# A state-space scan whose inputs come from TensorE, whose weighing by C is GpSimd's, and whose C is spread by DMA

## The reference, cut to what matters

```
Bx = xc @ B_w.T ; Cx = xc @ C_w.T            # 64 states each, per position
dt = softplus(xc @ dt_w.T + dt_b) + 0.0001
h  = exp(dt_t * A) * h + (dt_t * x_t) * Bx_t   # per position t, for all (d, n)
y  = einsum('bdn,bn->bd', h, Cx_t) + D_param * x_t
y  = y * silu(z)
```

## Time and profile before

| | us |
|---|---|
| median of 3 runs | 8258.76 (8253.63 to 8259.18) |
| the profiled execution | 8256.86 |
| its span | 8255.1 |
| TensorE busy in the span | 6220.3 (75%) |
| VectorE busy | 6656.1 (81%) |
| ScalarE busy | 3462.9 (42%) |
| GpSimd busy | 3679.6 (45%) |

### The profile page before, as it was taken

The page is one execution under the profiler, slowest core; times in us unless marked ns, Lnnn a source line. Parts: engine busy times, 40 slices in busy tenths (PEclk is TensorE's granted clock), DMA queues, the critical chain, the costliest instruction groups (busy, mean ns, idle before and its releaser), DMA issues. The chain is left out here.

```text
span 8255.1 us, 122802 instructions
## 1 busy us (share of the span) xinstructions
PE 6220.3 (75%) x40740; PEld 4162.2 (50%) x40740; DVE 6656.1 (81%) x11381; ACT 3462.9 (42%) x6666; POOL 3679.6 (45%) x1911
## 2 busy tenths in 40 slices
PE   5455555799966677777777777777778879999999
PEld 3355554577755422222222222222245558888888
DVE  6799998555557899999999999999955557676766
ACT  3333332333323566666666666666534421111121
POOL 0000000111100599999999999999822212222222
PEclk8777777899988899999999999999989989999999
DMA  2211111111022100000000000000011110000000
GB/s 64 73 43 43 43 43 52 43 37 37 28 79 108 66 15 15 15 15 15 15 15 15 15 15 15 15 15 15 12 57 46 40 63 8 7 8 8 7 8 6
DMA packets 335678, 254.48 MB, mean 31 GB/s; under 512 B 161763, under 2 KB 307046, under 8 KB 334854
## 3 DMA queue, kind: packets, MB, share of 16 engines
q1 hardware_dynamic: 332774, 248.29, 9.7%
q10 hardware_dynamic: 2464, 0.26, 0.0%
HBM read 140.46 MB, written 108.00 MB: 30 GB/s over the span
## 5 line engine op out<-in xcount | busy, mean ns | idle before, releaser
L1817 POOL TENSOR_TENSOR ss_inp<-ss_dx,ss_b_all 128x1024 f32<-128x1024 f32 x1024 | 2388.8, 2356 | 230.8 <-ACT ss_b_all L1791 229.0
L1835 DVE TENSOR_TENSOR_SCAN ss_h<-banks,ss_inp 128x1024 f32<-128x1024 f32 x1024 | 2313.1, 2278 | 59.7 <-ACT banks L1783 59.7
L1755 PE MATMUL banks<-ss_ch,ident 128*128 128x512 f32 x4096 | 1959.6, 601 | 64.9 <-DVE ss_xc L1851 64.9
L1733 PE MATMUL banks<-ss_bc,ss_pick 96*128 96x512 bf16 x2048 | 747.2, 386 | 787.9 <-DVE ss_ch L1844 750.4
L1783 ACT ACTIVATE banks<-ss_dt,ss_neg_a 128x510 f32<-128x510 f32 x2048 | 1334.7, 688 | 2.7 <-DVE ss_h L1835 2.7
L1791 ACT COPY ss_b_all<-banks 128x512 f32<-128x512 f32 x1024 | 599.3, 585 | 1236.5 <-PE banks L1733 1232.8
L1755 PEld LDWEIGHTS banks<-ss_ch,ident 128*128 128x128 f32 x4096 | 788.7, 193 | 635.1 <-issue 577.6
L1733 PEld LDWEIGHTS banks<-ss_bc,ss_pick 96*128 (+1 forms) x2048 | 200.0, 98 | 1662.7 <-issue 1484.7
L1844 DVE TENSOR_TENSOR ss_ch<-ss_h,banks 128x1024 f32<-128x1024 f32 x768 | 918.0, 1195 | 0.0
L605 PE MATMUL banks<-ms_rprod,ident 128*128 128x128 f32 x2048 | 467.0, 401 | 507.6 <-DVE ms_rprod L691 507.6
L2156 POOL TENSOR_TENSOR pk_blockhot<-pk_onehot,pk_parts 128x2048 bf16<-128x2048 bf16 x96 | 345.4, 3626 | 1101.0 <-DVE pk_parts L2394 1101.0
(11 more groups left out here) (293 smaller groups left out, 10281.1 us busy)
## 6 DMA issues: line engine op xcount, KB each, us to landing
keep_v<-ms_cx_values SPq DMA_DIRECT2D x32, 512.0 KB, 2.8
l_va<-keep_v SPq DMA_DIRECT2D x32, 512.0 KB, 5.3
l_kf<-keep_k SPq DMA_DIRECT2D x32, 256.0 KB, 2.9
keep_x<-l_x SPq DMA_DIRECT2D x32, 256.0 KB, 2.2
keep_xc<-si_xc SPq DMA_DIRECT2D x16, 512.0 KB, 2.7
keep_zs<-si_zs SPq DMA_DIRECT2D x16, 512.0 KB, 3.7
keep_dt<-si_acc SPq DMA_DIRECT2D x16, 512.0 KB, 2.6
keep_dx<-si_acc SPq DMA_DIRECT2D x16, 512.0 KB, 2.6
```

Source lines behind the costliest of these rows:

```text
L1733: T_.matmul(to[:, :], pick[:, bass.ds(n // 2, 1)].broadcast_to([ROWS, P]), inputs[i % 2][2][:, which, u % 2, :, :].rearrange("p g t -> p ( ...
L1755: m = T_.matmul(sums[j][:, :], chip.ident[:, :], ch[u][:, j, :], start=first, stop=False, skip_group_check=True)
L1817: G_.tensor_tensor(inp[u][:, :, :], inputs[i % 2][1][:, :, :, :].rearrange("p j g t -> p j (g t)"), rep(b_all[u][:, :], 1, HB), ALU.mult). ...
L1835: V.tensor_tensor_scan(flat(h[u][:, :, :]), decay[u % 2].rearrange("p j g t -> p (j g t)"), flat(inp[u][:, :, :]), 0.0, ALU.mult, ALU.add) ...
```

## The change

In `ssm_scan` a job is now one block of 128 channels, two sequences and two neighbouring states (NB = 2): again tiles of 128 x 1024, again 1024 jobs, in 8 groups of 32 blocks x 4 jobs (u is the channel block). The loop's body has 8 jobs.

- The inputs dx*B are made by TensorE. dx is stored turned (positions in partitions, `dxT`), and so is B (`bT`). ScalarE lays B's values on diagonals: `diag[t, n, t'] = ident[t, t'] * bT[t, n]`, two instructions of 128 x 128 a job, one block ahead. The product of dxT (stationary, 128 positions x 128 channels) with the two diagonals (256 columns) is dx*B for 128 positions, in PSUM. A job has four such products, for two sequences and two halves of the positions.
- The decays go to SBUF, in four buffers in place of two PSUM pairs.
- VectorE only scans, and applies D and the gate at a group's end.
- GpSimd multiplies every job's h by C. C is read from DRAM by a DMA per block that writes the same rows to all 128 partitions (512 KB each, 256 of them, two buffers). The spreading products, their copies and `pick` go away.
- TensorE's summing has the same two products of 512 columns a job, now with the moving side in two pieces of 256.

In `ssm_inputs` VectorE's five instructions on B and C go; TensorE projects C (64 x 256) and B turned (two times 128 x 64) apart and turns dx with 8 transposes a sequence; ScalarE makes four copies out of PSUM.

```diff
@@ ssm_inputs, vector
-        V.tensor_copy(z.bc[:, 0, :], src).then_inc(*own.up())
-        for part in range(2):
...
-            V.tensor_tensor(z.rest[:, part, :], src if part == 0 else z.rest[:, 0, :], z.bc[:, part, :], ALU.subtract
...
-            V.tensor_copy(z.bc[:, part + 1, :], z.rest[:, part, :]).then_inc(*(own.up() if part == 0 else (z.bc_ready.sem, 1)))
@@ ssm_inputs, scalar
+        A.copy(z.cn[:, :], bank[z.banks[0]][0:N, 0:T]).then_inc(z.bc_ready.sem, 1)
+        A.copy(flat(z.bT[:, :, :]), bank[z.banks[0]][:, T:T + NT * N]).then_inc(z.bc_ready.sem, 1)
...
+        for t in range(NT):
+            A.wait_ge(*z.dx_turned.at(i, t + 1))
+            A.copy(z.dxT[:, t, :], bank[z.banks[1 - t]][:, :]).then_inc(z.dxT_ready.sem, 1)
@@ ssm_inputs, tensor
-        project(T_, bank[z.banks[0]], blocks(wbc), blocks(z.xc)).then_inc(z.bc_projected.sem, 1)
+        for t in range(NT):
+            project(T_, bank[z.banks[0]], tiled(z.xc, t), [wbc[:, kt, 0:N] for kt in range(IB)], col=T + t * N)
+        project(T_, bank[z.banks[0]], [wbc[:, kt, N:] for kt in range(IB)], blocks(z.xc)).then_inc(z.bc_projected.sem, 1)
...
+                m = T_.transpose(bank[z.banks[1 - t]][:, j * P:(j + 1) * P], z.dx[:, j, t * P:(t + 1) * P], chip.ident[:, :])
@@ ssm_scan, tensor
+        def enter(i, k, u, slot):
+            group_loaded(T_, i, k, u)
+            T_.wait_ge(diag_made, number(i, k, UN))
+            after(T_, scanned, number(i, k, u) - 1)
+            for g in range(G):
+                for t in range(NT):
+                    m = T_.matmul(inp[u % 2][:, g, :, t * P:(t + 1) * P], inputs[i % 2][1][:, g, t, u * P:(u + 1) * P],
+                                  diag[slot][:, g, t, :, :].rearrange("p n t -> p (n t)"), start=True, stop=True)
+            m.then_inc(entered, 1)
 
         def total(i, k, u):
+            T_.wait_ge(weighed, number(i, k, u) + 1)
...
+            for n in range(NB):
+                m = T_.matmul(sums[u].rearrange("p (g t) -> p g t", g=G), chip.ident[:, :], ch[u][:, :, n, :], start=first and n == 0, stop=False,
+                              skip_group_check=True)
             m.then_inc(summed, 1)
...
+        def step(i, k, u, slot):
+            enter(i, k, u, slot)
+            if block_back(i, k):
+                total(*block_back(i, k), u)
@@ ssm_scan, scalar
+        def lay(i, k, u, slot):
...
+            for n in range(NB):
+                m = A.activation(diag[slot][:, g, t, n, :], chip.ident[:, :], ACT.Copy, scale=inputs[i % 2][2][:, g, t, bass.ds(k * NB + n, 1)])
+            m.then_inc(diag_made, 1)
 
         def decays(i, k, u):
             group_loaded(A, i, k, u)
+            after(A, scanned, number(i, k, u) - UN + 1)
+            for n in range(NB):
+                m = A.activation(decay[u][:, :, n, 1:T], inputs[i % 2][0][:, u, :, 1:T], ACT.Exp, scale=neg_a[:, u, bass.ds(k * NB + n, 1)])
@@ ssm_scan, gpsimd
+            if u == 0:
...
+                G_.wait_ge(c_loaded[slot], DMA * visits)
+            G_.wait_ge(scanned, m + 1)
+            after(G_, summed, m - UN + 1)
+            G_.tensor_tensor(ch[u][:, :, :, :].rearrange("p g n t -> p g (n t)"), h[u][:, :, :, :].rearrange("p g n t -> p g (n t)"), c_all[slot][:, :, :], ALU.mult
+                             ).then_inc(weighed, 1)
@@ ssm_scan, vector
+            V.wait_ge(entered, m + 1)
+            V.wait_ge(decayed, m + 1)
+            after(V, weighed, m - UN + 1)
+            V.tensor_tensor_scan(whole(h[u][:, :, :, :]), whole(decay[u][:, :, :, :]), whole(inp[u % 2]), 0.0, ALU.mult, ALU.add).then_inc(scanned, 1)
+            if i and fixed(k) and k == 0:
+                gate(i - 1, u)
@@ ssm_scan, sync
+    def load_c(S, i, k):
+        after(S, weighed, number(i, k - 1, 0))
+        S.dma_start(c_all[k % 2][:, :, :], dr["cn"][i * G:(i + 1) * G, NB * k:NB * (k + 1), :].rearrange("g n t -> g (n t)").unsqueeze(0).broadcast_to([P, G, NB * T])
+                    ).then_inc(c_loaded[k % 2], DMA)
```

More of the change, by code:

```diff
@@ L1676, in ssm_scan @@
[L1676 to L1682, removed]
@@ L1692, in number, with block_back, block_ahead @@
     def number(i, k, u):
[L1693 to L1700, removed]
+        return i * JOBS + k * UN + u
+    def block_back(i, k):
+        if fixed(k) and k == 0:
+            return (i - 1, BLOCKS - 1) if i else None
+        return i, k - 1
+    def block_ahead(i, k):
+        if fixed(k) and k == BLOCKS - 1:
+            return (i + 1, 0) if i + 1 < GROUPS else None
+        return i, k + 1
     def after(engine, sem, count):
@@ L1705, in after @@
             engine.wait_ge(sem, count)
[L1707 to L1711, removed]
     def blocks_of(engine, step):
@@ L1730, in tensor @@
     def tensor(T_):
[L1731 to L1736, removed]
-            group_loaded(T_, i, k, u)
[L1738 to L1747, removed]
+        def enter(i, k, u, slot):
+            group_loaded(T_, i, k, u)
+            T_.wait_ge(diag_made, number(i, k, UN))
+            after(T_, scanned, number(i, k, u) - 1)
+            for g in range(G):
+                for t in range(NT):
+                    m = T_.matmul(inp[u % 2][:, g, :, t * P:(t + 1) * P], inputs[i % 2][1][:, g, t, u * P:(u + 1) * P],
+                                  diag[slot][:, g, t, :, :].rearrange("p n t -> p (n t)"), start=True, stop=True)
+            m.then_inc(entered, 1)
@@ L1859, in step @@
-        def step(i, k, u):
-            if i and fixed(k) and k == 1 and u == 3:
-                gate(i - 1)
-            if back(i, k, u, 3):
-                scan(*back(i, k, u, 3))
-            if back(i, k, u, 4):
-                weigh(*back(i, k, u, 4))
-        blocks_of(V, step)
-        for n in range(3):
-            scan(*the_last(3)[n])
-            weigh(*the_last(4)[n])
-        weigh(*the_last(1)[0])
-        gate(GROUPS - 1)
-    def half(rows_, i):
-        return rows_.rearrange("p (j t) -> p j t", j=IB)[:, i % 2 * HB:(i % 2 + 1) * HB, :]
+            after(V, weighed, m - UN + 1)
@@ L1889, in sync, with store @@
+    def store(S, i):
+        for g in range(G):
+            S.dma_start(dr["ys"][i * G + g].rearrange("p (j t) -> p j t", j=IB), zs[:, :, g, :]).then_inc(ys_stored, DMA)
     def sync(S):
@@ L1919, in ssm_scan @@
     V.tensor_scalar(neg_a[:, :, :], neg_a[:, :, :], -1.0, None, ALU.mult)
-    G_.memset(pick[:, :], 0.0).then_inc(picked, 1)
-    for part in range(3):
-        G_.wait_ge(picked, part + 1)
-        G_.affine_select(out=pick[:, :], in_=pick[:, :], compare_op=ALU.not_equal, fill=1.0, base=-part * N // 2,
-                         pattern=[[-1, N // 2]], channel_multiplier=1).then_inc(picked, 1)
     for t in decay:
```

248 lines of the change are left out of this document (106 added, 142 removed).

## The result

The changed kernel takes 8587.88 us (median of 4 runs, 8581.08 to 8591.14) against 8256.19 before (8252.56 to 8259.18): ratio 1.0401, interval 1.0383 to 1.0419. The profiled execution took 8591.14 us with a span of 8589.4. The forecast was 8606.

The account below looks back on a forecast made before the run. VectorE sets the scan stage's pace at 3.112 us a job; the change makes TensorE the bound at 3.45. Terms 339 + 4 + 5 = +348 us on 8256.9 give a forecast of 8606 us, range 8560 to 8740.

Parts of the forecast that it names:

- TensorE becomes the bound at 3.45 us a job: Scan stage: eight entering records at 0.216 us plus four summing records at 0.430, above today's 3.112 us; +339 us.
- the rival in which they have four: Scan stage: entering products cost one record each, TensorE needs 2.58 us or less a job; 7490 to 7720 us, 3%.
- No wait of TensorE is late: Scan stage: what entries and summings wait for is long past, so the queue keeps TensorE full across the loop's branch.
- The rival with bubbles: Scan stage: TensorE bound, but the larger loop body loses 0.2 us a job; +205 us, 8810 us, 12%.
- The sum: Whole program: 339 for the scan stage, 4 for its cold start, 5 for `ssm_inputs`; +348 us.
- the cold start: Start of the scan stage: TensorE's first entries cost double for some 8 us; +4 us.
- `ssm_inputs` was put at +5: Stage before the scan: VectorE saves 29 us, TensorE gains 43 us; the middle of these bounds, +5 us.
- no table load: Scan stage, ScalarE: the rival had table reloads between exp and scaled copy, two of 1.283 us a job; 9580 us, 2%.
- C by DMA: Scan stage: each block's 512 KB load lands in 5 to 12 us, wanted after 13.8 us, so hidden.
- The prediction's edge: Scan stage: rival of late C decides from a 13.8 us landing; at 20 us +240 on the forecast, 8845 us, 3%.
- VectorE and GpSimd: Scan stage: VectorE falls to 2.28 us a job, GpSimd weighs every job at 2.36 us; neither is the bound.
- The sign: Whole program: slower 0.96, faster 0.03, same 0.01; it turns at 3.11 us a job on TensorE.

Follow-up runs that it names:

- The first experiment: Changed kernel with two of a job's four entering products done twice, output the same: 9470.81 us, ratio to before 1.1472.
- the fifth kernel: Changed kernel with VectorE adding the two weighed states up in every job, so TensorE sums one product instead of two: 7956.69 us, ratio 0.9636.
- the sixth: Changed kernel with additions of pairs dealt out: VectorE five in eight jobs, GpSimd two, one left to TensorE: 8074.97 us, ratio 0.978.
- the tenth: Changed kernel with one more VectorE multiplication of 128 x 512 a job before the scan, both inputs from SBUF, result unused: 8638.62 us.

## Why the prediction was right

*TensorE becomes the bound at 3.45 us a job.* Right: 3.44 measured, as 1.73 + 1.71. The step that decided is that a record's price was taken from the distance of records in a dense run, not from its duration. With the means of 601 and 380 ns a job would have come to 5.4 us and the program to 10.6 ms; with the records' busy time alone, 478 ns for 512 columns, to 3.8 us (1720.3/3595, and 482.0/2048 us for 256 columns on the page before). The first experiment gave 883 us for four more records a job, 0.216 us each. The entries have eight records a job (6504 for 813 jobs), so the rival in which they have four falls.

*No wait of TensorE is late.* Right, the groups show 0.0 us of idle time before either product. The rival with bubbles falls: a loop body of 8 jobs cost nothing. What the Trainium skill, "Runtime: NRT & Kernel Launch", section "Instruction fetch mechanics", says of a fetch after a taken branch has nothing to explain here; no run here shows a stall from one. The 131 ns for 512 columns of the Trainium skill, "TensorE: Matmul & The Clock Gate", section "Back-to-back issue gap", fall too: float32 records of that width start 0.43 us apart, and the bf16 ones of the kernel with bf16 sums 0.22 us, as the two of a job show there (start us, us):

```profile
4000.23 0.59 PE L1763 MATMUL banks<-ss_ch,identb 128*128 128x512 bf16 x2
4000.68 1.99 PE L1753 MATMUL banks<-ss_diag,ss_dxT 128*128 128x256 f32 x8
```

*The sum.* Forecast +348, measured +334 between the profiled spans. From the first entry at 2776.50 us to the last scan 3521.7 us pass, where the sum had 3522, and 3526 with the cold start. But it was held against 3183 us that count from the first scan; from there it is 3517.9, or +334.8. The cold start does show: the first 24 entering records take 8.19 us, (8.19 - 0.38)/23 = 0.34 apart in place of 0.216, 2.9 us more.

```profile
2776.50 8.19 PE L1753 MATMUL banks<-ss_diag,ss_dxT 128*128 128x256 f32 x24 [24.39 <-ACT ss_diag L1784]
```

It is hidden in the total because a job takes 3.443 us (the median distance of scans) and not 3.446, 3 us over the stage. No group end shows: 128 jobs take 440.7 us, which is 128 x 3.443. The first scan came 19.2 us after the stage's first instruction, where it took 20.6 before. `ssm_inputs` was put at +5 and shows -6, from one profile each. The old code had 432.9 and 429.8 us in two profiles, the new one 426.5 to 429.9 in eleven: a gain of a few us that these profiles don't settle. The middle between the two bounds was as good a guess as they allow.

*ScalarE.* Right: no table load, and busy 53% of the scan stage where I had said 55. The two scaled copies of a job are busy 0.68 us (553.7 us for 812 jobs); by distance, as the 0.54 was worked out, they take 0.59 (start us, us):

```profile
4002.39 1.32 ACT L1791 ACTIVATE ss_decay<-ss_dt,ss_neg_a 128x510 f32<-128x510 f32 x2
4003.61 0.68 ACT L1784 ACTIVATE ss_diag<-ident,ss_bT 128x128 f32<-128x128 f32 x2
4004.20 1.32 ACT L1791 ACTIVATE ss_decay<-ss_dt,ss_neg_a 128x510 f32<-128x510 f32 x2
```

The decays grew from 688 to 705 ns with SBUF as their target. ScalarE waited 1305 of 2800 us.

*C by DMA.* Right that it is hidden. The 512 KB land in 4.8 us, as the profile's page of the changed kernel says (KB, us to landing), and some 10 us more of delay cost nothing. The prediction's edge, "from a landing of 13.8 us on", was too early: C landed 14.4 us after its buffer was free and the time stayed. By the prediction's own formula for 20 us, the edge is where the landing and 4 x 2.36 us of weighing fill the 27.5 us of two blocks, at 18.1 us. No run tests that figure.

```profile
ss_c_all<-keep_cn SPq DMA_DIRECT2D x256, 512.0 KB, 4.8
```

*VectorE and GpSimd.* Harmlessly wrong. VectorE was put at 2.28 us for a scan; by distance it is 2.20. And I argued that GpSimd's 2.36 us hold beside any mix of VectorE's work, since two groups of rows agreed. They agreed because VectorE's 768 multiplications before had one input in PSUM, as the scans have in both kernels; only 32 at the group ends had both in SBUF. Neither touched the forecast. Durations in place of distances spoiled the expectation of the fifth kernel, and what contention costs VectorE those of the sixth and the tenth.

*The sign.* 3.11 us was the number to beat. By busy time a job, the change took 0.7 us of VectorE's 3.1 and 0.5 of GpSimd's 2.9, and brought TensorE from 2.3 to 3.4. Had its summing been cheaper, it would have been a gain: with pairs added first 3.6%, with bf16 sums 9.9%.

## What to carry to other kernels

Before work is moved off the busiest engine, add up what the receiving engine then has per unit of work, and compare it with the pace of today, not with the engine's share. Price TensorE by the distance from start to start in a dense run of the same width and type, and VectorE likewise. Where GpSimd works in SBUF, give VectorE's instructions beside it an input in PSUM, or count the wait. A float32 product with the identity that only adds is dear (0.86 us for 512 columns here); adding pairs on an idle VectorE (0.58 us) or rounding to bf16 where accuracy allows changes which engine is the pace.

## What the runs showed of the hardware

- A VectorE multiplication or addition with both inputs in SBUF and GpSimd's multiplication in SBUF hardly overlap: the second to start waits for the first. Where VectorE started first, GpSimd's 128x1024 multiplication ended 2.22 us (median) after VectorE's end, in the kernels with three jobs in four weighed or added by VectorE and in the tenth alike. So it went from 2.36 to 2.63 us beside an instruction of 0.69 us, and to 3.18 beside one of 1.20. Where GpSimd started first, it kept 2.36 us, and VectorE's 128x512 instruction ended 0.55 us after it, up to 2.85 us in place of 0.69. With one input in PSUM both kept their times, the scan included.
- VectorE's and GpSimd's records overlap their own engine's next by some 0.08 and 0.05 us when dense, so a duration overstates their price.
- A DMA of 512 KB that reads 4 KB of DRAM and writes it to 128 partitions lands in 4.8 us, no slower than a plain load of that size.
- TensorE at a granted clock of 0.54 from 3000 to 5800 us left VectorE's pace of 3.312 us from scan to scan as it was at 0.98 (the kernel before with sums in bf16, and without).
